# Where the last steps of a lane scan are computed: the guard's shift, the last rows' scaling, and two groups of sums

## The reference, cut to what matters

```python
xn = _layernorm(x)                      # x: (1, 2048, 128)
x  = x + attn0(xn) + expert(xn)         # attn0 returns xn + out, see below

# attn0: a recurrence over the tokens with a memory M (64 x 128)
def step(M, kv):
    v_pred   = k_t @ M
    surprise = norm(v_t - v_pred)
    M = M + eta * surprise * outer(k_t, v_t)
    return (M - mean(M)) * rsqrt(var(M) + EPS_LN), None
M, _ = scan(step, zeros, (k, v))
q    = phi(x_norm @ Wq.T)
out  = (q @ M) @ Wout.T                 # only the last M is used
attn0 = xn + out

# expert: relu(xn @ W1 + b1) @ W2 + b2, one expert of sixteen
```

## Time and profile before

| | |
|---|---|
| median of 3 runs | 259.81 us (258.69 to 259.90) |
| the profiled execution, first to last instruction | 258.2 us |
| TensorE busy | 245.4 us, 95% |
| VectorE busy | 206.3 us, 80% |
| ScalarE busy | 186.8 us, 72% |
| GpSimd busy | 112.7 us, 44% |
| mean granted clock of TensorE | 0.992 of full |

### The profile page before, as it was taken

How to read it: one execution, slowest core, us unless ns; L and a number is a source line. 1 busy time by engine, 2 the same in 40 slices (tenths; PEclk the granted TensorE clock), 3 DMA queues, 4 the chain that set the end, 5 groups by cost and what they waited for, 6 DMA issues and landing times.

```text
span 258.2 us, 5143 instructions
## 1 busy us (share of the span) xinstructions
PE 245.4 (95%) x1665; PEld 160.8 (62%) x1665; DVE 206.3 (80%) x694; ACT 186.8 (72%) x459; POOL 112.7 (44%) x148
## 2 busy tenths in 40 slices
PE   7798799999999999999999999999999999999993
PEld 2257554567674458688777767976975444444482
DVE  5998789999968898998899896897623897666684
ACT  1588499986637797887757899989923997777730
POOL 9698300000001689988655795987880000000000
PEclk9999799999999999999999999999999999999999
DMA  7720000000004704000000000000000000000004
GB/s 198 198 57 3 0 1 3 1 0 3 1 1 175 316 3 164 3 0 1 4 0 3 0 0 0 5 0 3 0 0 3 0 0 0 3 3 0 0 30 139
DMA packets 8303, 8.50 MB, mean 33 GB/s; under 512 B 1745, under 2 KB 7378, under 8 KB 7762
## 3 DMA queue, kind: packets, MB, share of 16 engines
q1 hardware_dynamic: 7442, 7.65, 9.1%
q10 hardware_dynamic: 832, 0.49, 0.7%
HBM read 7.09 MB, written 1.05 MB: 32 GB/s over the span
## 4 chain that ended last, share of the span: by engine, by line
PE 66%; DVE 16%; POOL 8%; ACT 4%; issue 3%; DMA 2%; DVEq 0%; SPq 0%; POOLq 0%; ACTq 0%
PE PS L930 11%; PE PS L929 11%; PE PS L902 8%; PE PS L879 7%; PE PS L892 4%; POOL arena L1461 4%; POOL arena L1462 3%; PE PS L693 3%; PE PS L646 3%; PE PS L701 2%; DMA x<-L_attn_x 2%; DVE mxb L1981 2%; DVE arena L1967 2%; PE PS L530 2%; PE PS L685 1%
## 5 line engine op out<-in xcount | busy, mean ns | idle before, releaser
L929 PE MATMUL PS<-arena 128*128 128x512 f16 x128 | 48.5, 379 | 0.0
L930 PE MATMUL PS<-arena 128*128 128x512 f16 x128 | 48.5, 379 | 0.0
L2039 DVE TENSOR_TENSOR arena<-arena 128x512 f32<-128x512 f32 x32 | 22.2, 693 | 13.0 <-ACT arena L1385 13.0
L879 PE MATMUL PS<-arena 128*128 128x512 f32 (+3 forms) x80 | 31.9, 530 | 0.3 <-ACT arena L1354 0.3
L1384 ACT ACTIVATE arena<-PS,arena 128x512 f32<-128x512 f32 x32 | 22.9, 716 | 9.1 <-PE PS L930 9.1
L1461 POOL TENSOR_TENSOR arena<-arena 128x256 f32<-128x256 f32 x32 | 21.6, 674 | 15.4 <-DVE arena L1973 12.9
L1354 ACT ACTIVATE arena<-PS,lnt 128x512 f32<-128x512 f32 (+3 forms) x40 | 24.8, 628 | 2.9 <-DVE lnt L1988 2.8
L1462 POOL TENSOR_TENSOR arena<-arena,small 128x256 f16<-128x256 f32 (+1 forms) x36 | 23.8, 662 | 2.8
L1469 POOL CAST arena<-arena 128x512 f16<-128x512 f32 x2 | 1.3, 636 | 54.3 <-ACT x L1247 54.3
L1385 ACT ACTIVATE arena<-PS,arena 128x512 f16<-128x512 f32 x32 | 22.8, 713 | 0.0
L1981 DVE TENSOR_REDUCE mxb<-PS 128x1 f32<-128x512 f32 (+3 forms) x40 | 22.1, 601 | 0.0
(11 more groups left out here) (291 smaller groups left out, 615.5 us busy)
## 6 DMA issues: line engine op xcount, KB each, us to landing
arena<-h_T SPq DMA_DIRECT2D x2, 1024.0 KB, 6.3
x<-L_attn_x SPq DMA_DIRECT2D x4, 256.0 KB, 4.7
arena<-cos SPq DMA_DIRECT2D x1, 1024.0 KB, 4.8
arena<-sin SPq DMA_DIRECT2D x1, 1024.0 KB, 7.8
arena<-w_T SPq DMA_DIRECT2D x3, 256.0 KB, 3.3
out<-arena SPq DMA_DIRECT2D x2, 256.0 KB, 2.2
con<-shape_constants ACTq DMA_DIRECT2D x1, 192.5 KB, 3.5
out<-arena SPq DMA_DIRECT2D x1, 192.0 KB, 2.0
```

The costliest lines, as they stand in the source:

```text
L879: i = mm(PS[:, k, 0:cnt * P], qT1[:, t * P:(t + 1) * P], kT1[:, c * P:(c + cnt) * P], start=True, stop=not last)
L929: mm(bank(b), wH[:, k, m * P:(m + 1) * P], sH[:, k, cols], start=(k == 0), stop=False)
L930: i = mm(bank(b), wL[:, k, m * P:(m + 1) * P], sL[:, k, cols], start=False, stop=(k == HT4 - 1))
L2039: v.tensor_tensor(RP[m], FP[m], high, ALU.subtract).then_inc(rest_ready, 1)
```

## The change

Five edits, all around the end of the lane chain:

- GpSimd adds `x` into `xn`, in four pieces of 128 x 512, each as soon as TensorE has transposed that piece of `xn`; then it adds `QE` into `QT`, eight pieces of 128 x 128. `expert_output` loses its matmul of `x` and waits for these sums, `memory_output` waits for the query sums by a new count. `query_sums` leaves VectorE.
- The reciprocal of the first norm and `c0`'s first 12 columns are computed behind steps 20 and 21 of the chain, TensorE shifts them behind step 24, and VectorE copies the shifted columns out of PSUM behind step 25. In the tail the subtraction reads that copy. Only the thirteenth column is shifted in the tail.
- ScalarE copies the fetched column out of PSUM and scales the last rows by it (`UW`), which VectorE did. The copy of `WVO`, which stood at the end of ScalarE's chain, moves behind step 18.
- TensorE counts the agreeing lanes ahead of the first memory products, not between them, and doesn't wait for the last scan ahead of fetching the column. Its products without use (`keep_warm`) stand behind steps 25 and 26, seven of them.
- Three small products are written to other PSUM banks.

```diff
+REST_AT, SHIFT_AT, WVO_AT = 20, 24, 18
@@ TensorE
-            def expert_output(c, first=0, end=7):
+            def expert_output(c, first=0, end=6):
                     if part == 0:
-                        mm(whole, ident, x[:, 4 * c:4 * c + 4, :]..., start=True, stop=False)
-                    elif part == 1:
-                        mm(whole, ident, xn[:, 4 * c:4 * c + 4, :]..., start=False, stop=False)
+                        pe.wait_ge(residual_ready, 2 + c + 1)
+                        mm(whole, ident, xn[:, 4 * c:4 * c + 4, :]..., start=True, stop=False)
...
-                    pe.wait_ge(q_ready, 2 * (4 * two + k + 1))
+                    pe.wait_ge(q_ready, 4 * two + k + 1)
...
-            for j in range(FAR + 1, L):
+            for j in range(FAR + 1, L - 1):
                 pe.wait_ge(scan_ready, j + 1)
                 if j in EO_AT:
                     expert_output(EO_AT.index(j) + 1)
-                elif EO_AT[-1] + 4 < j < L - 2:
-                    keep_warm(4, 4)
+                elif j == SHIFT_AT:
+                    pe.wait_ge(c0_ready, 1)
+                    mm(PS[0:W, 5, HALF:HALF + REST], ..., c0[0:W - 1, 0:REST], ...).then_inc(shift_done, 1)
+                elif j > SHIFT_AT:
+                    keep_warm(4 if j < L - 2 else 3, 4)
...
-            memory_output(0, 0, 2)
             pe.wait_ge(agree_ready, 1)
             mm(PS[0:1, 5, 1:2], agree, con[:, C_ONES:C_ONES + 1], ...).then_inc(count_done, 1)
+            pe.wait_ge(mw_act, 1)
+            memory_output(0, 0, 2)
@@ ScalarE
+                if j == WVO_AT:
+                    act.wait_ge(wvo_done, 1)
+                    f(WVO, PS[:, 7, 0:D], ACT.Copy).then_inc(wvo_act, 1)
...
-            act.wait_ge(wvo_done, 1)
-            f(WVO, PS[:, 7, 0:D], ACT.Copy).then_inc(wvo_act, 1)
+            act.wait_ge(last_act, 3)
+            act.wait_ge(gcol_done, 2)
+            n = o.did(f(gcol[0:2 * WINDOW], PS[0:2 * WINDOW, 6, HALF + 1:HALF + 2], ACT.Copy))
+            o.need(n)
+            f(UW..., U_LAST..., ACT.Copy, scale=gcol[0:2 * WINDOW]).then_inc(uw_ready, 1)
@@ GpSimd
+            for c in range(4):
+                piece = slice(4 * c, 4 * c + 4)
+                pool.wait_ge(xnt_done, c + 1)
+                tt(xn[:, piece, :], x[:, piece, :], xn[:, piece, :], ALU.add).then_inc(residual_ready, 1)
+            pool.wait_ge(qphi_act, 4)
+            for k in range(8):
+                part = slice(k * P, (k + 1) * P)
+                tt(QT[:, part], QT[:, part], QE[:, part], ALU.add).then_inc(q_ready, 1)
@@ VectorE, within the chain
-                    if j >= LATENT:
-                        query_sums(j - LATENT)
+                    if j == REST_AT:
+                        v.reciprocal(rh[:, 0:1], HS[:, REST:REST + 1]).then_inc(rh_ready, 1)
+                    if j == REST_AT + 1:
+                        v.scalar_tensor_tensor(out=c0[:, 0:REST], ...).then_inc(c0_ready, 1)
+                    if j == SHIFT_AT + 1:
+                        dve.wait_ge(shift_done, 1)
+                        did(v.tensor_copy(c0[:, 0:REST], PS[:, 5, HALF:HALF + REST]))
```

More of the change, by code:

```diff
@@ L181, in program @@
         rh, bound, agree = sc[:, 0:2], sc[:, 2:3], sc[:, 3:4]
-        rhb = sc[:, 6:7]
+        gcol, rhb = sc[:, 4:5], sc[:, 6:7]
         c0, c1 = take(REST + 1), take(L)
@@ L684, in expert_output @@
                     if part == 0:
-                        mm(whole, ident, x[:, 4 * c:4 * c + 4, :].rearrange("p n d -> p (n d)"), start=True, stop=False)
+                        pe.wait_ge(residual_ready, 2 + c + 1)
+                        mm(whole, ident, xn[:, 4 * c:4 * c + 4, :].rearrange("p n d -> p (n d)"), start=True, stop=False)
                     elif part == 1:
-                        mm(whole, ident, xn[:, 4 * c:4 * c + 4, :].rearrange("p n d -> p (n d)"), start=False, stop=False)
-                    elif part == 2:
                         mm(whole, warm[0:65, 0:P], b2parts[:, :].unsqueeze(1).broadcast_to([65, 4, D]), start=False, stop=False)
                     else:
-                        n = 4 * c + part - 3
+                        n = 4 * c + part - 2
                         for h in range(2):
@@ L711, in _ @@
             pe.wait_ge(eh_act, 8)
-            pe.wait_ge(b2_ready, 2)
-            expert_output(0, 1, 7)
+            pe.wait_ge(residual_ready, 2)
+            expert_output(0, 1, 6)
             pe.wait_ge(small_in, 16 * 13)
@@ L751, in _ @@
             mm(PS[:, 7, 0:D], UW, VW, start=True, stop=True).then_inc(mw_done, 1)
-            pe.wait_ge(c0_ready, 2)
-            mm(PS[0:W, 5, HALF:HALF + REST + 1], con[0:W - 1, C_ID + 1:C_ID + 1 + W], c0[0:W - 1, :], start=True, stop=True).then_inc(shift_done, 1)
+            pe.wait_ge(agree_ready, 1)
+            mm(PS[0:1, 5, 1:2], agree, con[:, C_ONES:C_ONES + 1], start=True, stop=True).then_inc(count_done, 1)
             pe.wait_ge(mw_act, 1)
             memory_output(0, 0, 2)
-            pe.wait_ge(agree_ready, 1)
-            mm(PS[0:1, 5, 1:2], agree, con[:, C_ONES:C_ONES + 1], start=True, stop=True).then_inc(count_done, 1)
             def general():
@@ L1695, in _ @@
             last()
-            def query_sums(*pieces):
-                dve.wait_ge(qphi_act, 4)
-                for q in pieces:
-                    part = slice(q * P // 2, (q + 1) * P // 2)
-                    v.tensor_tensor(QT[:, part], QT[:, part], QE[:, part], ALU.add).then_inc(q_ready, 1)
             formed = added = o.n
```

42 lines of the change are left out of this document (21 added, 21 removed).

## The result

The changed kernel takes 268.64 us in the median of 6 executions (267.38 to 269.82), the kernel before beside it 259.86. The ratio is 1.032, with a 95% interval of 1.0282 to 1.0358. It is slower, as forecast, but by 8.8 us and not by 3.6: outside the range.

What follows compares the result with a forecast made beforehand. VectorE was taken to bound steps 0 to 13, the VectorE-ScalarE hand-over those from about 19, the guard the tail. The sum + 4.8 - 1.1 - 0.1 = + 3.6 us on 259.8 gave 263.4 us, range 258.5 to 265.5.

Steps and rivals of the forecast that it cites:

- the tail's term: Behind the last scan: earlier flag and memory product gain 1.1 us, between 0.3 and 1.4; statistics 3.5 after the scan.
- The hold: Early chain steps, from 37: GpSimd's two-operand sums block VectorE's two-operand instructions, costing 4.8 us.
- three adds that count: Early chain: GpSimd's 512-column adds of x after the first each hold VectorE 1.01 us, 3 x 1.01.
- eight query sums: Early chain: GpSimd's eight 128-column adds each hold VectorE 0.28 us, 8 x 0.28.
- The first add: Ahead of 38.33: GpSimd's first add of x falls into VectorE's idle 0.77 us and costs nothing.
- The sign for step 0: Start of the chain: step 0's scan would stand near 42 in place of 39.07.
- The rival without a hold: Early chain: VectorE's two-operand sums pass GpSimd's, so only tail and chain count: -1.2, 258.6 us; chance 0.21.
- the one that slips into gaps: GpSimd's sums wait for later gaps in steps waiting for ScalarE; 2.4 less 1.2, 261.0 us; chance 0.13.
- More than the stall: Early steps: TensorE idles, its clock falls, 1 to 2 us more, 265 us; within the forecast's 0.66 as upper part.
- the memory product would be late next: Tail: first two memory banks finish at 76.2, later than flag and branch at 76.11, so they release the statistics.
- the guard: Tail path from the last root to the flag, the later one before; its flag was forecast 1.35 us earlier, at 74.80.
- Within the chain: Steps 18 to 27: query sums leave VectorE, small new instructions come; 0.1 us gained, between 0 and 0.5.

Runs made afterwards that it cites:

- e3: The changed kernel with eight more products without use in TensorE's two pauses ahead of the last scans; 267.17 us, ratio 1.0222 to 1.0301.
- e13: e3 with sixteen more products without use, placed where TensorE is idle near steps 0 to 2, ahead of its wait; 265.42 us, ratio 1.0154 to 1.0270.
- e8: e3 with the query sums back on VectorE, so GpSimd does only the four two-operand sums of x; 263.61 us, ratio 1.0062 to 1.0159.
- e16: The changed kernel run once more for a second trace; 269.37 us, one run.
- e12: e3 run once more for a second trace; 267.04 us, one run.
- e9: The changed kernel with the addition of x left out altogether and the query sums on VectorE; 260.57 us, ratio 0.9989 to 1.0045.
- e5: e3 with 21 more products without use, put behind TensorE's wait for ScalarE's first hidden rows; 267.28 us, ratio 1.0197 to 1.0353.
- e10: e9 with the eight products without use of e3 in its pauses; 259.64 us, ratio 0.9965 to 1.0017.
- e7: e1 with ScalarE's copy of WVO put back behind the loop; 259.57 us, ratio 0.9931 to 0.9988.
- e11: e1 without query sums in the two steps forming the shift's factors, and with ScalarE's copy of WVO in step 26; 259.52 us, ratio 0.9956 to 1.0008.
- e6: e1 with the eight query sums alone given to GpSimd, x still added by TensorE; 261.37 us, ratio 1.0013 to 1.0085.
- e1: The changed kernel with its GpSimd sums taken back, leaving the tail edits alone; 259.65 us, ratio 0.9957 to 1.0005 of the kernel before.
- e15: The kernel before with eight products without use in TensorE's pauses near 24 and 27; 258.86 us, ratio 0.9919 to 0.9975.
- e14: e1 with eight products without use in TensorE's pauses near 24 and 27; 258.36 us, ratio 0.9902 to 0.9948.

## Why the prediction was wrong

The step that failed is the tail's term, with the overlap it rests on. The prediction put the tail at -1.1 us with TensorE at full clock, and counted it as a gain that TensorE is ahead of the chain at step 24. Measured is +0.87 for the tail and +1.27 behind it, beside 10 us at half clock; with the clock at 1.00 the tail is as forecast (e3, e13).

*The hold.* The mechanism and the size were right: 4.8 forecast, 4.50 measured. Its parts: three adds that count, 3.03, measured 2.64 to 2.85 (e8); eight query sums, 2.24 less VectorE's 0.48, measured 1.86 and, alone, 1.67. The single adds were longer than taken (5.25 for four instead of 4.64), probably since VectorE holds GpSimd up too, as in the earlier trace rows. The first add did fall into the idle 0.77. The sign for step 0 (its scan near 42) didn't come: it stood at 39.80, and 3.77 of the 4.50 were lost in steps 1 and 2. The rival without a hold and the one that slips into gaps are refuted by the rows at 37 to 46.

*More than the stall.* This rival named the right mechanism, and was mis-sized: it gave TensorE's clock 1 to 2 us and only the early steps. The early steps cost 0.44 in the profiled execution, 0.85 in e16 and 1.8 in e12. The fall in the tail was not in it. It should have been: the prediction saw that TensorE, relieved of the matmul of `x`, "is ahead of the chain at step 24", counted that as a gain, and didn't ask what TensorE does while it is ahead. It pauses. The 2.1 us between the changed kernel's 5.56 and e3's 3.46, and 1.0 of the 1.27 in the second layer (e3: 181.07), stand beside this clock; the other 0.3 has no cause here. That the pauses alone don't cost it rests on one trace (e9), and what the hold adds is open.

*The tail.* Forecast -1.1, measured +0.87. Only the clock was wrong here: where TensorE stays at 1.00 with short banks, the statistics come 3.45 to 3.51 behind the last scan (e3, e5, e8, e9, e10, e13), forecast 3.5, and the flag 2.02 and 2.03 (e13, e3), forecast 2.0. That the memory product would be late next holds for e3, e5, e12 and e13, by a little: the statistics start 1.43 behind the flag, where before, with the guard the later one, it was 1.31. In e8, e9 and e10, whose flag comes at 2.20, it is 1.30, so there the guard is still the later one. (The traces put the wait down to the memory product in every kernel, before included, so that the distance to the flag has to tell.) At half clock it is 2.48.

*Within the chain.* Forecast -0.1, measured +0.64: two waits at steps 23 and 25 that no row of before showed. e7 and e11 tie step 25's to where ScalarE's copy of `WVO` stands. For the 0.37 at step 23, which comes in after, e3, e5, e6, e12, e13 and e16, all with the new tail and without query sums on VectorE, no cause was tried.

*The sum.* 4.50 + 0.44 + 0.64 + 0.87 + 1.27 = 7.7 in the span against 3.6. Of the 4.1 between, 2.0 are the tail, 0.7 the chain's late steps, 0.4 step 14 and 1.3 the second layer, less 0.3 of the hold. The range was too narrow at the top because the upper end took the clock as one lengthening of one stage, and not as something that can fall again at TensorE's later pauses. The working has two slips that carry nothing: by its own terms ScalarE's scaling ends at 73.64, not at 73.75, and the chances split into 0.11 faster, 0.16 the same and 0.73 slower, not 0.12, 0.17 and 0.71.

## What to carry to other kernels

Before a sum goes to an idle GpSimd, look at what VectorE does then: if its instructions have two SBUF operands and set the pace, GpSimd's two-operand instructions cost the chain half their length here (4.50 of 9.04 us), while a one-operand form of the residual cost a third of what its two-operand form did (0.95 against 2.85). Before taking work from TensorE, look at where it will pause: a product that was "in the way" may be what kept its clock. Here shorter banks cost no clock alone in the trace of e9, and together with the hold they went with 10 us of half clock, in the tail and the second layer. And fill pauses where TensorE is idle already, ahead of its wait (e13), not behind it (e5).

## What the runs showed of the hardware that was not expected

- The spread of the kernel before goes with TensorE's clock. Its 38 executions beside e1 to e8 come in three groups: mean granted clock 0.996 to 0.997 with spans of 257.0 to 257.1, 0.991 to 0.993 with 258.0 to 258.5, and 0.986 to 0.987 with 259.3 to 259.8. With the pauses near 24 and 27 filled (0.72 and 1.40 us before) the spread is gone (e15: spans of 256.9 to 257.1; with the tail edits, e14: 256.3 to 256.7).
- GpSimd's scalings with one tensor operand lasted 0.97 each beside the chain, 0.79 in the first stage (6 in 4.74), and cost VectorE 0.95 in 15.6 us.
